# Position-wise expert mixture: 64 positions per stationary and half the output columns per unit, against 32 positions and whole blocks

## The reference

```python
x = jnp.transpose(hidden_states, (1, 0, 2))
h = relu(jnp.einsum('bsh,oh->bso', x, gW1) + gb1)
g = (jnp.einsum('bsh,eh->bse', h, gW2) + gb2).mean(axis=1)
W1 = jnp.einsum('be,eoi->boi', g, eW1);  b1 = g @ eb1
W2 = jnp.einsum('be,eoi->boi', g, eW2);  b2 = g @ eb2
y = relu(jnp.einsum('bsi,boi->bso', x, W1) + b1[:, None, :])
y = jnp.einsum('bsi,boi->bso', y, W2) + b2[:, None, :]
```

## Time and profile before

| | us |
|---|---|
| median of three runs | 2796.37 (2793.72 to 2798.17) |
| span of the profiled execution | 2792.1 |
| stage `position_experts`, first matmul to last apply2 | 452.87 to 812.14 |
| from there to the next stage's first instruction | 18.3 |
| PE busy, whole span | 2517.8 (90%) |
| DVE busy | 1702.0 (61%) |
| ACT busy | 1391.3 (50%) |
| mean granted TensorE clock | 0.964 of 2.4 GHz |

### The profile page before, as it was taken

The page is one execution under the profiler, slowest core; times in us unless marked ns, Lnnn a source line. Parts: engine busy times, 40 slices in busy tenths (PEclk is TensorE's granted clock), DMA queues, the critical chain, the costliest instruction groups (busy, mean ns, idle before and its releaser), DMA issues. The chain is left out here.

```text
span 2792.1 us, 84762 instructions
## 1 busy us (share of the span) xinstructions
PE 2517.8 (90%) x36489; PEld 2135.0 (76%) x36489; DVE 1702.0 (61%) x3422; ACT 1391.3 (50%) x3486; POOL 733.8 (26%) x1078
## 2 busy tenths in 40 slices
PE   7999888999968999999998859978997878999988
PEld 6888656777756899999987659977776656999577
DVE  6877675666656333333335755657885777777663
ACT  4888324455532444444432324427884454777342
POOL 3222102212102300000001213423446535666300
PEclk9999999999989999999999969988999999999999
DMA  3110003212031100000000043334320003111000
GB/s 97 36 36 21 1 4 94 63 33 63 3 87 47 36 17 17 17 17 17 2 2 25 4 150 101 127 108 141 93 66 1 2 2 99 48 53 49 1 1 31
DMA packets 118228, 126.76 MB, mean 45 GB/s; under 512 B 10877, under 2 KB 110152, under 8 KB 117864
## 3 DMA queue, kind: packets, MB, share of 16 engines
q1 hardware_dynamic: 114024, 110.93, 13.0%
q0 software_dynamic: 3840, 10.49, 1.2%
HBM read 105.67 MB, written 15.73 MB: 43 GB/s over the span
## 5 line engine op out<-in xcount | busy, mean ns | idle before, releaser
L1157 ACT ACTIVATE s_ca_probs<-s_ca_scores,s_ca_neg_max 128x256 f32<-128x256 f32 x768 | 353.4, 478 | 35.0 <-DVE s_ca_neg_max L1203 25.7
L1203 DVE TENSOR_REDUCE s_ca_neg_max<-s_ca_scores 128x4 f32<-128x1024 f32 x192 | 233.8, 1219 | 46.1 <-PE s_ca_scores L1056 24.7
L2212 DVE COPY s_mx_w_mixed<-s_mx_ps 128x512 f32<-128x512 f32 x256 | 163.7, 684 | 93.5 <-PE s_mx_ps L2058 80.0
L1073 PE MATMUL s_ca_probs_flipped<-identity,s_ca_probs 128*128 128x128 f32 x1536 | 210.6, 280 | 1.7 <-ACT s_ca_probs L1157 1.7
L1073 PEld LDWEIGHTS s_ca_probs_flipped<-identity,s_ca_probs 128*128 128x128 f32 x1536 | 164.4, 141 | 40.2 <-issue 20.8
L2167 ACT COPY s_mx_w_mixed<-s_mx_ps 128x512 f32<-128x512 f32 x256 | 137.4, 589 | 106.6 <-PE s_mx_ps L2045 86.0
L1157 ACT ACTIVATION_READ_ACCUMULATOR s_ca_probs<-s_ca_scores,s_ca_neg_max 128x1 f32 x768 | 160.5, 209 | 0.0
L1164 ACT COPY s_ca_probsT<-s_ca_probs_flipped 128x512 f32<-128x512 f32 x192 | 115.4, 601 | 77.4 <-PE s_ca_probs_flipped L1073 77.3
L971 POOL TENSOR_TENSOR s_ca_inv_spread<-s_ca_inv_sums,h_ca_own_half 128x128 f32<-128x128 f32 x192 | 72.6, 399 | 287.2 <-DVE s_ca_inv_sums L1225 287.2
L82 PE MATMUL s_cc_shared<-s_cc_ctxT_low,h_cc_wkv_high 128*128 128x256 f32 x512 | 146.0, 285 | 2.2 <-DVE s_cc_ctxT_low L1556 2.2
L300 POOL TENSOR_SCALAR x_normed_transposed<-x_normed_transposed,h_cc_rstd,h_cc_shift 128x256 f32<-128x256 f32 x56 | 30.6, 556 | 446.1 <-PE s_cc_out L1450 271.1
(11 more groups left out here) (571 smaller groups left out, 7561.2 us busy)
## 6 DMA issues: line engine op xcount, KB each, us to landing
h_ca_ctxT<-in_ctxT SPq DMA_DIRECT2D x96, 256.0 KB, 3.4
h_mx_w_by_input<-in_L_ffn_eW1T SPq DMA_DIRECT2D x16, 512.0 KB, 5.6
h_mx_w_by_hidden<-in_L_ffn_eW2T SPq DMA_DIRECT2D x8, 1024.0 KB
h_re_win<-in_L_ffn_W_in SPq DMA_DIRECT2D x8, 1024.0 KB, 6.0
h_ca_ctx<-in_ctx SPq DMA_DIRECT2D x32, 256.0 KB, 2.8
x_normed_transposed<-in_ctx SPq DMA_DIRECT2D x7, 1024.0 KB, 5.3
h_re_wout<-in_L_ffn_W_out SPq DMA_DIRECT2D x8, 512.0 KB, 3.8
choice_results<-s_rt_zeros SPq DMA_DIRECT2D x4, 1024.0 KB, 10.6
```

Of the source, the lines that this page charges most:

```text
L1073: last = nc.tensor.transpose(psT[u % len(psT)][:, 2 * a + c, :], PR[b % 2][:, 4 * n + 2 * h + a, c * P:(c + 1) * P], ident[:, :])
L1157: last = nc.scalar.activation(PR[b % 2][:, p, :], psS[:, p // 2, (p % 2) * NKEY:(p % 2 + 1) * NKEY], ACT.Exp, bias=nmax[b % 2][:, p:p + 1] ...
L1203: nc.vector.tensor_reduce(nmax[b % 2][:, 4 * n:4 * n + 4], psS[:, 2 * n:2 * n + 2, :].rearrange("p r (g k) -> p r g k", g=GR), AX_X, ALU.m ...
L2212: last = nc.vector.tensor_copy(part(int(name[1]), r), bank(j, r))
```

## The change

`position_experts` is rewritten; nothing outside it changes. A unit u is now all 64 positions with half the output columns (64 of a block's hidden columns for W1, 128 of the 256 outputs for W2). Each block has four units: two for W1 (u % 4 is 0 or 1) and two for W2 (2 or 3), and there are NU = 32. Within a unit, a quarter n is 16 positions for the applies and flips.

- A mix job M has 8 matmuls with 256 moving columns (64 positions by 4 outputs) in place of 16 with 128. It takes two of three pairs of PSUM banks. It waits until the first copies of the mix before it are done on ACT and on DVE.
- All other jobs use one bank each, two banks in turn, in quarters: apply1 has 32 matmuls with 64 moving columns, apply2 has 16 with 128, turns and flips 4 transposes.
- The bias of a quarter is four matmuls, all from the same row group (32 n), into one bank. Before, four such matmuls used four different row groups and four banks.
- The mixes of unit u + 1 stand between the applies of unit u. ACT empties A, F and T1, DVE empties Y and T2; mixes are shared as before.
- The store and fetch of Y go by halves of the columns, 512 B a row in place of 1 KB, and the last half in two pieces. The last addition to X is shared by DVE and POOL.

```diff
+    def quarters(u):
+        jobs = []
+        if u % 4 == 2:
+            jobs.append(("F", u - 1, 3))
+        for n in range(NQ):
+            jobs.append(("A" if u % 4 < 2 else "Y", u, n))
+            if u % 4 == 0:
+                jobs.append(("T2", u // 4, n))
+            if u % 4 == 1 and n >= 1:
+                jobs.append(("F", u, n - 1))
+            if u % 4 == 2 and u // 4 + 1 < OB:
+                jobs.append(("T1", u // 4 + 1, n))
+        return jobs
...
-        S = [ps("mx_ps", [P, 4, 512]) for _ in range(2)]
+        MIXED = [sb("mx_mixed", [P, SEQ * P]) for _ in range(2)]
+        PAIR = [ps("mx_mix_ps", [P, 2, 512]) for _ in range(3)]
+        SM = [ps("mx_small_ps", [P, 512]) for _ in range(2)]
...
+        def order(u):
+            mixes = [("M", u + 1, n) for n in range(NQ)] if u + 1 < NU else []
+            smalls = quarters(u)
+            out = mixes[0:1]
+            n = 0
+            for j in smalls:
+                if j[0] in ("A", "Y") and n:
+                    out += mixes[n:n + 1]
+                out.append(j)
+                n += j[0] in ("A", "Y")
+            return out
...
+                sp.wait_ge(s_small_dve, emptied(BY_DVE, PLACE[("Y", NU - 2, 3)]))
+                store(0, slice(0, SEQ), 0)
+                sp.wait_ge(s_back[0], 16)
+                fetch(0, slice(0, SEQ))
                 for h in range(2):
-                    store(h)
-                    fetch(h)
+                    sp.wait_ge(s_small_dve, emptied(BY_DVE, PLACE[("Y", NU - 1, 2 * h + 1)]))
+                    store(1, slice(32 * h, 32 * h + 32), h + 1)
+                for h in range(2):
+                    sp.wait_ge(s_back[h + 1], 16)
+                    fetch(1, slice(32 * h, 32 * h + 32))
...
+                def mix(u, n):
...
+                    if m >= 1:
+                        pe.wait_ge(s_mix_act, 2 * m - 1)
+                        pe.wait_ge(s_mix_dve, 2 * m - 1)
+                    for q in range(2):
+                        for r in range(4):
+                            rows = slice(32 * r, 32 * r + 32)
...
+                            last = nc.tensor.matmul(PAIR[(2 * m + r // 2) % 3][:, r % 2, q * 256:(q + 1) * 256], w,
+                                                    GB[rows, :, :, :].rearrange("p k s o -> p (k s o)"), start=True, stop=True)
...
+                def gates(g, r):
+                    return GR[32 * r:32 * r + E, g * GS:(g + 1) * GS, :].rearrange("p s b -> p (s b)")
+
+                def apply1(u, n):
...
+                    for i in range(4):
+                        nc.tensor.matmul(dst[:, i * OH:(i + 1) * OH], gates(4 * n + i, n), EB1[32 * n:32 * n + E, at:at + OH], start=(i == 0), stop=False)
+                    for i in range(4):
+                        for c in range(KC):
+                            for q in range(GS):
+                                s = (4 * n + i) * GS + q
+                                last = nc.tensor.matmul(dst[32 * q:32 * q + 32, i * OH:(i + 1) * OH], XNT[:, c, s * BATCH:(s + 1) * BATCH],
+                                                        mixed1(u)[:, c, s, :], start=False, stop=(i == 3 and c == KC - 1))
...
+                dve.wait_ge(s_here[1], 64)
+                nc.vector.tensor_tensor(X[:, 0:10, DH:DIM], X[:, 0:10, DH:DIM], YX[:, 0:10, DH:DIM], ALU.add).then_inc(s_x, 1)
```

More of the change, by code:

```diff
@@ L1929, in position_experts @@
     OB = DFF // P
-    HS = SEQ // 2
+    NU = 4 * OB
+    NQ = 4
     GS = 4
[L1932 to L1960, removed]
+    OH, DH = P // 2, DIM // 2
@@ new lines, in quarters @@
+    def quarters(u):
[11 more added lines that the diff above has]
+        return jobs
+    SMALL = [("T1", 0, n) for n in range(NQ)] + [j for u in range(NU) for j in quarters(u)]
@@ L1978, in _, with store, fetch @@
             def _(sp):
[L1979 to L1987, removed]
+                def store(h, rows, piece):
+                    to = back[h, rows.start * BATCH:rows.stop * BATCH].rearrange("(g p) n -> p g n", p=P)
+                    g = slice(rows.start // GS, rows.stop // GS)
+                    sp.dma_start(to, Y[:, g, h * DH:(h + 1) * DH]).then_inc(s_back[piece], 16)
+                def fetch(h, rows):
+                    got = back[h].rearrange("(s t b) n -> b s t n", b=2, t=TILES)
                     for b in range(2):
-                        sp.dma_start(YX[b * SEQ + h * HS:b * SEQ + (h + 1) * HS, :, :], rows[b, h * HS:(h + 1) * HS]).then_inc(s_here, 16)
+                        sp.dma_start(YX[b * SEQ + rows.start:b * SEQ + rows.stop, :, h * DH:(h + 1) * DH], got[b, rows]).then_inc(s_here[h], 16)
                 for ob in range(1, OB):
@@ new lines, in _, with mixed, hidden, flipped @@
+            def _(act):
+                def mixed(u, n):
+                    act.wait_ge(s_mix, 4 * u + n + 1)
+                    for r in (0, 2):
+                        nc.scalar.copy(part(u, n, r), bank(u, n, r)).then_inc(s_mix_act, 1)
+                def hidden(u, n):
+                    e = PLACE[("A", u, n)]
+                    act.wait_ge(s_small, e + 1)
+                    to = HS_[:, 4 * n:4 * n + 4, u % 2 * OH:(u % 2 + 1) * OH]
+                    nc.scalar.activation(to, SM[e % 2][:, 0:4 * OH].rearrange("p (g o) -> p g o", o=OH), ACT.Relu).then_inc(s_small_act, 1)
+                def flipped(u, n):
+                    e = PLACE[("F", u, n)]
+                    act.wait_ge(s_small, e + 1)
+                    nc.scalar.copy(HT[:, 4 * n:4 * n + 4, :].rearrange("p a b -> p (a b)"), SM[e % 2][:, :]).then_inc(s_small_act, 1)
+                def turned1(ob, n):
+                    e = PLACE[("T1", ob, n)]
+                    act.wait_ge(s_small, e + 1)
+                    nc.scalar.copy(W1L[:, 2 * n:2 * n + 2, :].rearrange("p a c -> p (a c)"), SM[e % 2][:, :]).then_inc(s_small_act, 1)
+                run = {"M": mixed, "A": hidden, "F": flipped, "T1": turned1}
+                for n in range(NQ):
+                    turned1(0, n)
+                for n in range(NQ):
+                    mixed(0, n)
+                for u in range(NU):
+                    for kind, v, n in order(u):
+                        if kind in run:
+                            run[kind](v, n)
```

357 lines of the change are left out of this document (129 added, 228 removed).

## The result

| | before | after |
|---|---|---|
| median, us | 2796.65 (4 runs) | 2857.07 (4 runs, 2853.32 to 2865.23) |
| ratio | | 1.0215, 95% interval 1.0198 to 1.0232 |
| span of the profiled execution, us | 2792.1 | 2852.2 |
| start of the stage's matmuls | 452.87 | 453.63 |
| first matmul to last apply2 | 359.3 | 407.1 |

The change makes the kernel slower, as forecast, but by 60 us and not by 32. The median lies 1 us above the range. The profiled executions differ by the same 60.1 us: of these, 0.8 are ahead of the stage, 47.8 in it, 3.4 at its end and 8.1 behind it, in stages whose source the change does not touch.

The account below looks back on a forecast made before the run. PE was taken to bound the stage. Work +60, switch -3, waits -26 and end +1 gave +32 us: profiled span 2792.1 to 2824, median 2828, range 2803 to 2856.

Parts of the forecast that it names:

- Work on PE: PE's jobs in the stage: 47.0 us a block, 384 with the first block's bias, 60 more than before, less 3.
- the switch: PE going from mix to bias, both taken as 32-row, 128-column stationaries: perhaps free, 3 us off, bounds 0 and 6.
- The bias: Apply1's bias on PE: 8 records in sequence at 0.11, 1.02 us a job against 0.44, 6.4 more a block.
- The waits: PE's waits in the stage, mainly for emptied PSUM: 9 us against 35, 26 less.
- One wait is new: In units with u % 4 = 2 the first turn waits for the last flip's bank: 0.37 x 7 = 3 us.
- The start: Stage's first unit, before the first bias at about 465.2: 7.2 us of jobs done in 12.3, so 5 us waited.
- The end: From last addition to Y through store, fetch and last addition to X: 17.5 us against 16.5, +1; bounds 7.4 and 21.
- The rest of the program: Stages behind the changed one: the forecast's sum had no term for them.
- the two signs of being wrong: In the stage: a block under 45 us, or PE's idle time as long as before, would show the prediction wrong.
- The bias paced by its moving columns: Rival on apply1's bias: 0.055 us a record, job 0.58, 2797 us in all, no change; 13%.
- Loads that do not overlap in one row group: Rival on the bias matmuls: load and matmul in sequence, job 1.46, 2863 us in all; 5%.
- The rival with the waits: Rival on PE's waits: two small banks turn as slowly as two halves, 26 us come back, 2854; 10%.

Follow-up runs that it names:

- run 1: Changed kernel without the expert bias of apply1 (the four matmuls of a quarter): 2811.50 us, ratio 1.0046 to the kernel before.
- run 4: Kernel before, with the four bias matmuls of an apply1 all on row group 0: 2815.84 us, ratio 1.0064 to the kernel before.
- run 6: Changed kernel with apply1's bias as one matmul a quarter and apply2's bias added to X by token on POOL: 2825.25 us, ratio 1.0097.
- run 2: Changed kernel with turn quarters behind the four applies as 2, 1, 1, 0 in place of 1, 1, 1, 1: 2844.95 us, ratio 1.0159.
- run 7: Changed kernel with bias as one matmul and by token, turns as 2, 1, 1, 0, and the end's stores and addition reordered: 2810.85 us, ratio 1.0041.

## Why the prediction was right in its sign and wrong in its size

**Work on PE** was forecast as 384 - 3 = 381 us. By the measured prices a block is 8 x 0.98 + 8 x 1.08 for mixes, 8 x 0.92 + 8 x 1.04 + 8 x 1.01 for bias and applies, 12 x 0.585 for turns and flips, 47.3; eight, and apply2's eight biases (0.98 each), are 385.9. Right within 5. Inside the term two things were off: the bias took 0.10 less than forecast in all 64 places, where 3 us were taken off for the switch, and a mix ahead of an apply costs 1.08, near the upper bound of 1.10, and not half an apply2. (The bias's stationary has 8 rows, not the 32 that the passage on the switch gives it.)

**The bias** decided, as said: 0.92 a job against 1.02 forecast. Runs 1, 4 and 6 take it away, put it into the old kernel, and shorten it, and each moves the stage by the bias's price, within 3 us.

**The waits** are the step that failed: "In all 9 against 35, 26 less." The stage held 407.1 - 385.9 = 21.2. The prediction asked when PSUM is emptied, for mixes, applies, turns and flips, and concluded "One wait is new". It did not ask when the mix's stationary is there. The order puts the first mix of the next-but-one unit right behind the last turn quarter, whose copy it reads: 8 x 0.85 + 7 x 0.75 = 12 us (the eighth wait of the latter kind is in the start), which run 2 takes out. The one new wait that was named, of a turn for the last flip's bank, took 0.16 at a time (652.84 to 654.01 is 1.17, against 1.01), six times, 1 us in place of 3. The start waits 5, as forecast, but in this profile the clock falls to 1.2 GHz behind it: 3.1 more, unforeseen. Together these are 21.1 of the 21.2.

**The end** was forecast as +1 and came to +3.4. Counted as the prediction counts, from the last addition to Y to the end of the last addition to X, 16.5 us became 20.4 (861.47 to 881.91), against 17.5 taken and an upper bound of 21. Left out were POOL's share of the last addition, 1.7 us longer than DVE's, and the slower first store, 6.0 in place of 4.5.

**The rest of the program** was taken as unchanged, without a look at what a stage passes on to the next; its 8.1 us were in no term. It is true that no source outside `position_experts` changes, but the new stage's semaphores move the barriers behind it, and some 4 of the 8 us stand at one of them. Work 4.9, waits 12.2, ahead of the stage 0.8, end 2.4, rest 8.1: together the 28 us between 32 and 60. Had only one of the two large misses happened, the waits or the rest, the time would have stayed inside the range. Neither of the two signs of being wrong came (a block took 49.2 us, and PE's idle time fell by 11): they could not tell 9 us of waits from 21.

**The rivals.** The bias paced by its moving columns is refuted: 0.92, not 0.58. Loads that do not overlap in one row group are refuted as well: 0.92, not 1.46. The Trainium skill's rule in "TensorE: Matmul & The Clock Gate", "Part 3: Packing small matmuls — row/col tiling", does not hold for these eight records of one row group either. The rival with the waits named the right term and the wrong mechanism: not the banks, which run 2 leaves as they are, but the turns' copies. That its 2854 lies near 2857 is luck: of its 26 us the waits hold 12, and the rest came from terms that it did not name.

## What to carry to other kernels

For every job that is moved, list each operand that it waits for, the stationary's copy as well as the free bank, and look at what stands directly ahead of it; a producer one place ahead of its reader costs its whole copy. Price the smallest repeated job first: four matmuls that stood beside each other in four row groups cost more than twice as much in one (0.44 against 1.05). Halving jobs to shorten waits pays for each cut with a fixed part, which in run 7 took some 20 of the 25 us that the waits gave. And ask what a stage hands on besides its data: here the number of its semaphores moves barriers in stages that nobody edited.

## What the runs showed of the hardware that was not expected

- What follows a mix costs up to 0.1 us of PE: the same mix, of 32-row stationaries, takes 1.08 ahead of a 128 x 32 stationary and 0.98 ahead of an 8 x 128 one (run 1, and the changed kernel). The Trainium skill, "TensorEngine Tiling (Array Packing)", "Key Properties", says that changing the tiling mode drains TensorE; the rows fit this, with 0.1 us as the price, if the 8-row stationaries count as the mode of the 32-row ones, which no run here shows.
- POOL adds 128 x 768 float32 in 3.10 us while, at the same time, DVE adds 128 x 1280 in 1.49: 3.5 times as long per column.
- The first store of Y, half the columns of all positions in rows of 512 B, took 6.0 us to its fetch (5.1 to 6.3 in the six profiles with this order); the last store before, half the positions in rows of 1 KB, took 4.5 in all four profiles of the old stage.
- The same 23772 matmul records behind the stage took 1961.6 to 1977.1 us in the profiled runs, at a granted clock of 0.96 over the whole of it in the kernel before and 0.95 in the changed one.
